# The order of all engines' calls in a four-block gated attention and mixture kernel

## The reference

```
x = x + tanh(g_xattn[0]) * cross_attention_0(layernorm(x), ctx)   # A: two softmax attentions, x to ctx and ctx-side, mixed by a sigmoid gate
x = x + tanh(g_ffn[0])   * moe_top1(layernorm(x))                 # B: softmax router over 8 experts, one 256x256 matrix of the best one
x = x + tanh(g_xattn[1]) * attention_1(layernorm(x), ctx)         # C: 16 heads of 16, rotary q and k, output projection
x = x + tanh(g_ffn[1])   * moe_top2(layernorm(x))                 # D: 8 experts of 256 to 128 to 256 with gelu, two best ones weighted
```

## Time and profile before

| | us |
|---|---|
| median of three runs | 514.29 (513.15 to 519.85) |
| the profiled execution | 510.58 |
| its span, first to last instruction | 509.3 |
| TensorE busy in it | 470.3 |
| VectorE, ScalarE, GpSimd busy | 356.2, 339.3, 272.5 |
| mean granted clock of TensorE | 0.97 |

### The profile page before, as it was taken

How to read it: one execution, slowest core, us unless ns; L and a number is a source line. 1 busy time by engine, 2 the same in 40 slices (tenths; PEclk the granted TensorE clock), 3 DMA queues, 4 the chain that set the end, 5 groups by cost and what they waited for, 6 DMA issues and landing times.

```text
span 509.3 us, 11112 instructions
## 1 busy us (share of the span) xinstructions
PE 470.3 (92%) x3918; PEld 409.2 (80%) x3918; DVE 356.2 (70%) x897; ACT 339.3 (67%) x691; POOL 272.5 (53%) x337
## 2 busy tenths in 40 slices
PE   3999999999999987589977699999999999999996
PEld 3899999989988877567745388698797978788896
DVE  6757876698636657957657878776774786975485
ACT  3587888748675633353264698888778768688843
POOL 2425563665624186764477767837666454432264
PEclk9999999979999995699999899999999999999999
DMA  7899200011456532779838160230500503000001
GB/s 206 287 352 363 105 23 2 23 62 63 126 156 194 188 107 86 221 204 310 246 119 266 43 217 17 100 93 1 170 23 3 190 22 127 26 2 24 1 23 41
DMA packets 41975, 61.51 MB, mean 121 GB/s; under 512 B 5198, under 2 KB 22976, under 8 KB 41920
## 3 DMA queue, kind: packets, MB, share of 16 engines
q1 hardware_dynamic: 36064, 52.67, 32.3%
q0 software_dynamic: 1536, 4.20, 2.7%
q10 hardware_dynamic: 4320, 3.93, 2.3%
HBM read 26.21 MB, written 17.43 MB: 86 GB/s over the span
## 4 chain that ended last, share of the span: by engine, by line
PE 71%; DVE 7%; POOL 6%; issue 5%; ACT 4%; DMA 4%; SPq 2%; POOLq 0%; ACTq 0%; DVEq 0%
PE psum L389 16%; PE psum L391 14%; PE psum L390 14%; PE psum L627 5%; PE psum L556 5%; PE psum L598 4%; PE psum L396 4%; PE psum L615 3%; ACT PT L1381 2%; DMA st<-parts 2%; POOL yg L2828 2%; PE psum L557 1%; SPq L3075 1%; PE psum L636 1%; DVE mpad L2261 1%
## 5 line engine op out<-in xcount | busy, mean ns | idle before, releaser
L2261 DVE TENSOR_REDUCE mpad<-psum 128x4 f32<-128x1024 f32 x64 | 76.7, 1219 | 22.0 <-PE psum L598 20.5
L1381 ACT ACTIVATE PT<-psum 128x1024 f32<-128x1024 f32 x64 | 64.2, 1024 | 20.6 <-PE psum L615 18.0
L2800 POOL TENSOR_TENSOR wA<-stage,wA 128x512 fp32r<-128x512 f32 x32 | 41.3, 1291 | 53.4 <-ACT wA L1428 50.9
L2330 DVE SCALAR_TENSOR_TENSOR xall<-psum,gat,xall 128x256 f32<-128x256 f32 x112 | 46.6, 476 | 7.1 <-PE psum L391 3.9
L389 PE MATMUL psum<-wB,wA 128*128 128x256 f32 x128 | 38.7, 302 | 0.1
L389 PE MATMUL psum<-x4h,wB 128*128 128x256 f32 x128 | 37.6, 294 | 0.0
L627 PE MATMUL psum<-PT,vv 128*32 128x256 f32 x512 | 35.1, 393 | 1.3 <-ACT PT L1381 1.3
L390 PE MATMUL psum<-wB,wA 128*128 128x256 f32 x128 | 35.9, 281 | 0.0
L391 PE MATMUL psum<-wB,wA 128*128 128x256 f32 x128 | 35.9, 280 | 0.0
L391 PE MATMUL psum<-x4h,wB 128*128 128x256 f32 x128 | 35.8, 279 | 0.0
L390 PE MATMUL psum<-x4l,wB 128*128 128x256 f32 x128 | 35.7, 279 | 0.0
(11 more groups left out here) (283 smaller groups left out, 1754.8 us busy)
## 6 DMA issues: line engine op xcount, KB each, us to landing
st<-parts SPq DMA_DIRECT2D x48, 256.0 KB, 3.0
wt<-exp_d SPq DMA_DIRECT2D x30, 256.0 KB, 2.8
slots_d<-ys SPq DMA_DIRECT2D x3, 2304.0 KB
stage<-mats_d SPq DMA_DIRECT2D x21, 256.0 KB, 3.9
cx<-ctx_d SPq DMA_DIRECT2D x16, 256.0 KB, 3.3
xs<-slots_d SPq DMA_DIRECT2D x30, 128.0 KB, 3.0
y_d<-ys ACTq DMA_DIRECT2D x30, 128.0 KB, 3.1
qr<-qp SPq DMA_DIRECT2D x28, 128.0 KB
```

The costliest lines, as they stand in the source:

```text
L1381: e.activation(PT[:, i:i + 2, :, :].rearrange("p a k n -> p (a k n)"), ps2("ST", b, j).rearrange("p a n -> p (a n)"), ACT.Exp, scale=0.25) ...
L2261: e.tensor_reduce(mpad[:, :, 0:16].rearrange("p t (o a) -> p t o a", a=8)[:, :, :, j], ps2("max", b, j).rearrange("p o (t n) -> p t o n", ...
L2330: e.scalar_tensor_tensor(out=xall[:, b, t, :], in0=ps("dn", b, x)[:, t * 256:(t + 1) * 256], scalar=gat[:, b % 2, t, x:x + 1], in1=xall[:, ...
L2800: e.tensor_tensor(hlo[:, i, :], stage[:, n % 4, :], hh[:, i, :].bitcast(F32), ALU.subtract).then_inc(h_lo, 1)
```

## The change

All five lists are written in another order. No helper changes, and each list holds the same calls as before. For TensorE a call may also write another PSUM bank than before (its last argument). Behind batch 4 of block C fewer calls move, and most lines of TensorE's diff there only change a bank. Where a call only changed its bank it does not count as moved. In batch 6 of block C, ACT adds the bias of the keys ahead of that of the queries, as in all other batches. The core of the diff, by engine:

```diff
@@ TensorE @@
 
             fold(0, 0)
-            ln_T("A", 0, 1)
-            fold_g(0, 2)
+            fold_g(0, 1)
+            ln_T("A", 0, 2)
             proj("t0", 0, 3)
             proj("vc", 0, 0)
             scores(0, 0, 1)
             fold(1, 2)
...
-            moe_T(14, 2)
+            ln_T("B", 5, 1)
+            moe_T(14, 3)
             moe_w(13)
             moe_w(14)
             rank(4, 0)
-            gate(7, 1)
+            route_B(5, 1)
+            gate(7, 2)
+            rank(5, 0)
+            mix(7, 1)
+            c_k(0, 2)
             ln_T("B", 6, 0)
-            c_k(0, 2)
-            route_B(6, 0)
-            mix(7, 1)
-            rank(5, 2)
-            rank(6, 3)
+            route_B(6, 1)
             ln_T("B", 7, 0)
             ln_T("C", 0, 1)
-            route_B(7, 2)
-            c_q(0, 0)
-            rank(7, 1)
-            c_v(0, 2)
-            ln_T("C", 1, 0)
+            route_B(7, 3)
+            rank(6, 0)
+            c_q(0, 2)
+            rank(7, 0)
+            c_v(0, 1)
+            ln_T("C", 1, 2)
+            c_q(1, 0)
             c_k(1, 1)
-            c_v(1, 0)
-            c_q(1, 1)
-            moe_T(15, 2)
+            c_v(1, 2)
+            moe_T(15, 1)
             moe_T(16, 3)
             moe_w(15)
...
+            c_exp(4, 0, 6)
             c_PV(1, 0)
-            c_exp(4, 0, 6)
             c_exp(5, 0, 4)
             c_exp(6, 0, 6)
             c_exp(7, 0, 4)
             c_PV(2, 0, 1)
             c_max(7, 1, 6)
             c_PV(3, 0)
-            c_maxT(1, 0)
-            c_out(0, 2, 1)
-            c_outT(0, 3)
-            c_v(3, 1)
+            c_v(3, 0)
+            c_out(0, 1, 2)
+            c_maxT(1, 3)
+            c_outT(0, 0)
             c_max(0, 2, 4)
@@ ScalarE @@
             store_tile(14)
             gate_t(7)
             x_hi("B", 6)
             top_exp(5)
-            k_bias(0)
             ln_apply("B", 7)
+            top_exp(6)
             ln_apply("C", 0)
             x_hi("B", 7)
+            k_bias(0)
             x_hi("C", 0)
-            top_exp(6)
             q_bias(0)
+            ln_apply("C", 1)
             ctx_hi("C", 1)
-            v_copy(0)
-            ln_apply("C", 1)
             x_hi("C", 1)
             part_hi(1, 0)
+            v_copy(0)
             part_hi(0, 0)
             k_bias(1)
+            xs_T(15)
             q_bias(1)
-            xs_T(15)
+            xs_T(16)
             ln_apply("C", 2)
...
+            store_tile(26)
             store_tile(25)
-            store_tile(26)
+            k_bias(3)
+            store_tile(27)
             xs_T(29)
-            store_tile(27)
             st_exp(0, 0)
+            st_exp(1, 0)
             store_tile(28)
-            st_exp(1, 0)
             store_tile(29)
             part_hi(0, 2)
             st_exp(2, 0)
             st_exp(3, 0)
-            k_bias(3)
             q_bias(3)
             st_exp(4, 0)
             st_exp(5, 0)
+            o_copy(0, 0)
             st_exp(6, 0)
             st_exp(7, 0)
-            o_copy(0, 0)
             o_copy(1, 0)
+            v_copy(3)
+            ctx_hi("C", 4)
             o_hi(0)
             ln_apply("C", 4)
-            ctx_hi("C", 4)
             st_exp(0, 1)
             part_hi(1, 3)
             st_exp(1, 1)
+            st_exp(2, 1)
             w_hi("f3")
-            w_hi("f0")
-            st_exp(2, 1)
             st_exp(3, 1)
             st_exp(4, 1)
             w_hi("f2")
             w_hi("f1")
+            w_hi("f0")
             st_exp(5, 1)
             x_hi("C", 4)
             st_exp(6, 1)
             ln_apply("D", 0)
             o_copy(0, 1)
...
             x_hi("C", 7)
+            k_bias(6)
             q_bias(6)
-            k_bias(6)
             ln_apply("D", 2)
@@ VectorE @@
             a_stats(7)
-            rcp(0, 4)
+            mixed(3)
             x_lo("A", 5)
-            mixed(3)
             rcp(1, 4)
+            slots(0)
             P_lo(0, 4)
-            slots(0)
+            proj_lo("t0", 5)
             proj_lo("vc", 4)
             P_lo(1, 4)
+            b_top(1)
+            proj_lo("t1", 5)
             gate_B(0)
-            b_top(1)
-            proj_lo("t0", 5)
-            proj_lo("t1", 5)
             slots(1)
             proj_lo("vs", 5)
+            gate_B(1)
             row_max(0, 5)
...
             slots(4)
+            w_lo("wv")
+            b_top(5)
             gated(7)
-            gate_B(5)
+            slots(5)
+            gate_B(4)
             mixed(7)
             add_moe(0)
             c_stats(0)
+            gate_B(5)
             b_top(6)
-            slots(5)
-            slots(6)
+            gate_B(6)
             add_moe(1)
             c_stats(1)
             x_lo("C", 0)
-            gate_B(6)
+            slots(6)
             b_top(7)
-            add_moe(2)
             slots(7)
             alloc(1)
+            add_moe(2)
             turned(1)
+            x_lo("C", 1)
+            c_stats(2)
             turned(0)
-            x_lo("C", 1)
             add_moe(3)
-            c_stats(2)
+            y_out(15)
             c_stats(3)
-            y_out(15)
@@ GpSimd @@
             ln_rstd("B", 3)
             scatter(0)
             ctx_lo("A", 6)
             out_lo(0, 4)
+            sum_diff(4)
             scatter(1)
-            sum_diff(4)
             out_lo(1, 4)
+            scatter(2)
             ln_rstd("A", 7)
             scatter(3)
-            scatter(2)
+            w_lo("r")
             out_lo(0, 5)
@@ SyncE @@
+            load("ks")
             load_ctx("A", 0)
-            load("ks")
             load("vs")
             load("vc")
             load_x(2)
             tables()
-            load_ctx("A", 1)
             load("kc")
             load("qs")
             load_x(1)
-            load_x(4)
             load("g1")
             load("g0")
+            load_ctx("A", 2)
             load_x(3)
+            load_x(4)
+            load_ctx("A", 1)
...
             load_tile(7)
+            load("f1")
             load_tile(8)
-            load_ctx("C", 1)
+            load("f3")
+            load("f0")
             load_tile(9)
             load_tile(10)
             load_tile(11)
+            load_ctx("C", 1)
             load_tile(12)
-            load_ctx("C", 2)
             load_tile(13)
             load_tile(14)
-            load("f3")
+            swap_half(1, 0)
+            load_ctx("C", 2)
             load("f2")
-            swap_half(1, 0)
             swap_half(0, 0)
+            load_tile(18)
             load_tile(16)
+            load_tile(15)
             load_tile(17)
-            load_tile(15)
-            load_tile(18)
             stack(0)
             swap_halves(1)
             load_tile(19)
             load_tile(20)
             load_tile(21)
+            load_ctx("C", 3)
             load_tile(22)
-            load_ctx("C", 3)
             load_tile(23)
             load_tile(24)
             load_tile(25)
             stack(1)
             load_tile(26)
+            swap_halves(2)
             load_tile(27)
-            swap_halves(2)
             load_tile(28)
             load_tile(29)
-            load("f0")
             max_rows(0)
             load_ctx("C", 4)
```

942 lines of the change are left out of this document (466 added, 476 removed).

## The result

The changed kernel took 511.88 us (median of 20 executions, 507.34 to 515.14) against 515.21 for the one before (20 executions beside it on the same chip): a ratio of 0.9939, 95% interval 0.9916 to 0.9963. That is 3.3 us less than the kernel before beside it (by the ratio 3.1 us of the 514.29 of the forecast), where 7.0 was forecast. The direction and the range held, the size did not.

What follows compares the result with a forecast made beforehand. The pool was taken as 24.6 us of TensorE idle time and 13.5 us of half clock, outside the full stage. Terms of -7.5 with 0.5 taken off gave -7.0: 514.29 to 507.3 us, range 500.0 to 515.5.

Steps and rivals of the forecast that it cites:

- 178 to 216 us: End of the first phase: earlier scatter(7) 1.0, C1's order and first tile's copy 1.0; -2.0 us, bounds -8.4 and +3.
- 216 to 296 us: Tiles and first attention: shorter ACT chain, earlier stack(2), one exponential put into a wait; -3.0 us, bounds -8 and +1.5.
- Start and the counts of batch 1: Earlier loads at the start, -0.3 us; at 101.8 to 116.0, TensorE's 0.7 us wait and a third of the clock, -2.2.
- the bound of this step: At 101.8 to 116.0, the upper bound of +1.2 us: another full GpSimd operation falling on another small one.
- that shorter longest gap may keep the clock up: At 178.2 to 216.0, c_k(0) behind mix(7) fills as much of the 5 us waiting there; no size of its own.
- third rival: Clock falls between gate(7) and mix(7), scatter(7) 3 us late if route_B(6) ends after 193.7; 517.3 us, chance 0.10.
- The seventh batch's keys: In the full stage, ACT's query bias waits 1.4 us for the keys' products, x_hi ahead of both; 0, bounds 0 and +0.8.
- the rest: The remainder of 296 to 509 us: 0, bounds -1.2 and +1.5 us.
- The base: Whole kernel: -7.0 us taken from the profiled execution of 510.58 us, carried over to the median of 514.29 us.
- the signs named: Right: one-hot waits within 1 us, half clock under 25, C1's ln_T 1 us sooner, stack(2) by 267.5. Wrong: new waits or half-clock stages.

Runs made afterwards that it cites:

- r13: The changed kernel a third time, in group 4, against the kernel before: ratio 0.9944, median 512.23 us.
- r9: The new order with c_k(0) moved between rank(5) and mix(7), in group 3, against the kernel before: ratio 0.9915, median 507.25 us.
- r14: The new order with c_k(0) between rank(5) and mix(7) once more, in group 4, against the kernel before: ratio 0.9894, median 509.08 us.
- r3: The changed kernel once more, for a second profile, against the kernel before: ratio 0.9933, median 513.30 us.
- r2: New order up to about 210 us (SP up to the eighth tile), old order behind it, against the kernel before: ratio 0.9981, median 514.88 us.
- r6: The new order with plain DMAs in place of all 16 indirect gathers, against the kernel before: ratio 0.9848, median 509.38 us.
- r4: The kernel before once more, unchanged, for a second profile: ratio 0.9999, median 516.83 us.
- r5: The old order with plain DMAs in place of all 16 indirect gathers, against the kernel before: ratio 0.9843, median 507.90 us.
- r11: The old order with plain DMAs in place of the gathers of batches 0 to 3, against the kernel before: ratio 0.9979, median 510.58 us.
- r17: The old order with plain DMAs in place of the gathers of batches 4 to 7, against the kernel before: ratio 0.9946, median 508.97 us.
- r12: The new order with plain DMAs in place of the gathers of batches 0 to 3, against the kernel before: ratio 0.9986, median 512.34 us.
- r18: The new order with plain DMAs in place of the gathers of batches 4 to 7, against the kernel before: ratio 0.9953, median 508.76 us.
- r7: The old order up to about 210 us, the new order behind it, against the kernel before: ratio 0.9984, median 515.77 us.
- r8: The kernel before with one edit, the bias of the seventh batch's keys ahead of its queries' on ACT: ratio 0.9999, median 515.73 us.

## Why the forecast was right or wrong, by its own steps

Two terms failed: 178 to 216 us (forecast -2.0, measured +0.3) and 216 to 296 us (forecast -3.0, measured -0.3). The same points in the profiles, in us (old: two; new: two; third, of r13, full clock 5 us late; c_k(0) moved: r9 and r14):

| | old | new | r13 | r9, r14 |
|---|---|---|---|---|
| moe_T(0) | 135.0, 135.0 | 133.2, 133.2 | 136.9 | 133.0, 133.2 |
| transposes of C1 | 209.2, 209.7 | 207.9, 208.0 | 213.2 | 206.1, 206.7 |
| st_exp(0, 0) | 258.8, 258.5 | 254.9, 257.5 | 261.9 | 254.0, 255.8 |
| st_exp(0, 2) | 311.2, 313.5 | 310.5, 310.5 | 315.9 | 305.9, 308.8 |
| end | 509.3, 511.5 | 508.5, 508.6 | 513.9 | 504.0, 507.3 |

- *Start and the counts of batch 1, -0.3 and -2.2.* -1.8 at moe_T(0), near the 2.5. The mechanism is as told, with the shares turned round: up to moe_T(0) half clock cost 3.4 us before and nothing in the first profile of the changed kernel, and TensorE's idle time rose from 10.0 to 10.8 us. The half clock went: none in r3 and r9 either, 3.4 us in r2, r6 and r13, against 6.8 in every profile of the old order. The wait did not: it moved to the counts of a later batch (1.86 at 114.83), and for the reason given as the bound of this step, another full GpSimd operation on another small one:

```profile
111.02 0.96 POOL L2817 DMA_INDIRECT slots_d<-xB,slot  x1 [0.30 <-issue]
112.01 1.28 POOL L2765 TENSOR_TENSOR cs1l<-cf,cs1h 128x512 fp32r<-128x512 f32 x1
...
111.58 1.75 DVE L2039 TENSOR_SCALAR sm<-sm 128x2 f32<-128x2 f32 x1
```

  The small operation ends at 113.33, when GpSimd's ends (113.29). By the Trainium skill, "SBUF — State Buffer", section "SBUF: two separate sides", the second comer is blocked for the whole instruction. The two ends agree with it; that VectorE's row begins 0.43 us ahead of GpSimd's, beside an indirect scatter, leaves open who came first.
- *178 to 216, -2.0: the first step that failed, by its mechanism.* The clause "that shorter longest gap may keep the clock up" is the wrong one: half clock began sooner and lasted longer. From moe_T(0) to C1's transposes, with TensorE's idle time and the price of half clock (half of the busy time that lies in it):

| | us | idle | price of half clock |
|---|---|---|---|
| old: before, r4 | 74.2, 74.7 | 8.7, 10.9 | 6.0, 4.1 |
| old, gathers replaced: r5, r11, r17 | 73.3, 73.3, 74.3 | 7.8, 7.8, 8.8 | 6.0, 6.0, 6.0 |
| new: first, r3, r13 | 74.6, 74.8, 76.3 | 7.9, 7.9, 7.9 | 7.1, 7.2, 8.9 |
| new, gathers replaced: r6, r12, r18 | 76.3, 74.8, 74.8 | 7.9, 7.9, 7.9 | 8.9, 7.2, 7.2 |
| c_k(0) moved: r9, r14 | 73.0, 73.5 | 9.0, 9.3 | 3.9, 4.1 |

  Less both, 59.5 to 60.1 us are left in each of the thirteen profiles, so these two account for the lengths. The new order took idle time off (0.8 us against the first profile, 3.0 against r4, whose idle time holds the late increments) and paid for it with half clock, 23.9, 27.3 and 30.7 us of it against 20.5 and 17.0 (stretches that begin in the stage). What brings it is in the forecast's third rival (with nothing between gate(7) and mix(7) the clock falls before c_k(0) and route_B(6)); I had priced that as all or nothing, deciding at 193.7. route_B(6) ended at 191.0, well before that, so the rival's 3 us did not come, but its half clock did. With the wait filled the price falls by 3.1 to 3.2 us for 1.1 to 1.4 us more of idle time: r9 and r14 are 1.4 us faster here than the first two profiles of the new order, and 1.2 faster than the old, not the full 2.0 of the forecast. The Trainium skill, "TensorE: Matmul & The Clock Gate", section "Part 1: The HAM clock gate", has idle time take the clock down; the trace agrees in part. Here a wait of 1.79 us in a thinly filled stretch was followed by half clock within 1 us of its end in the first profile, r3, r12 and r18. It is not the whole cause: in r13 and r6 a first half-clock stretch of 3.4 us began 6.6 us before the end of that wait, and in r2, with the same wait, half clock came only at 191.9, 5.4 us behind it:

```profile
186.48 0.66 PE L512 MATMUL psum<-ident,uu 128*128 128x128 f32 x4 [1.79 <-DVE uu L2056]
```

- *216 to 296, -3.0: the second step that failed; what took it is open.* One part came as forecast. From the first exponential to the issue of stack(2) it was 10.21 us and is 8.76 (263.69): 1.45 sooner, forecast 1.5, and 5.3 in all with what came before. But from C1's transposes to st_exp(0, 2) the old profiles take 102.0 and 103.8, the new ones 102.6, 102.6 and 102.7, so -0.3 in the mean is what is left of -3.0. In the changed kernel there are the 3.61 us of wait, beside the gathers, and 6.8 us of half clock from 267.9, for which the forecast has no term. They are not shown to be what took the gain: where no profile of either order has a late increment, the same piece takes 98.2 us old and 98.7 new (r5, r6), 103.0 and 102.7 (r11, r12), 99.2 and 99.0 (r17, r18), so there the gain is no larger. r7, the new order from 216 on alone, gave nothing either. In the first profiles stack(2) is issued 5.3 us sooner and st_exp(0, 2) starts only 0.7 sooner.
- *The seventh batch's keys, 0*, and *the rest, 0*: right (r8; 198.0 to 198.1 us from st_exp(0, 2) to the end in the two old and three new profiles).
- *The base.* "510.58 - 7.0 = 503.6 ... 514.29 - 7.0 = 507.3 by the same difference" took the profiled execution for a typical one. It had 30.7 us at half clock and no late increment; its kernel's mean was 41 to 43 on three chips and 32 to 33 on a fourth. So the profiles of old and new differ by 0.8 and 2.9 us (1.9 between the means of the first two each), and the medians by 3.3: some of the measured gain lies in what my one profile could not show, and for that part the forecast's sign was luck. The late mix(7) and rank(5), which three profiles of the old order (r4, r7, r8) have at 188 to 196, are a part of it that I can name, but did not isolate; in the three profiles of the changed kernel the reader of mix(7) starts at once (185.96 in the first, behind 185.92).

Of the signs named: the start of the C1 transposes, stack(2) and the full stage came as for a right forecast; a wait for the counts over 1 us, 39.2 us at half clock in the profile instead of under 25, and half clock in 178 to 192 and 262 to 277 came as for a wrong one.

The terms sum to -7.5; the first two profiles of each order show -1.8 + 0.3 - 0.3 = -1.8. Over the whole span TensorE's idle time was 39.0 and 39.7 us in them, and is 36.7 and 37.8 (37.0 in r13): 2.1 us off, 2.2 with r13, less than a third of the forecast. Half clock cost 13.5 and 15.6 us, and costs 15.4 and 14.0 (18.9 in r13), where the forecast counted on less.

The version with c_k(0) in the wait is 4.1 us (r9) and 5.9 us (r14) faster than the kernel before, by the medians, and 3.2 us faster than the changed kernel on the one chip that timed both.

Open: what in an indirect DMA holds TensorE's increments back, and why on some chips; what took the 3.0 us of 216 to 296; the changed kernel on the chip that shows no late increments (the three pairs of orders with gathers replaced say 0.2 us faster to 1.8 us slower than the old one by the medians, but none is the kernel itself); and what the pause at 265 costs, since r17 and r18 met a chip without it.

## What to carry to other kernels

Split every execution into time at half clock and the rest before and after a reordering. An order that packs the idle time of a thin stretch can make TensorE's clock fall earlier, and each us of half clock in which TensorE is busy gives back half a us (27.0 of 30.7 us before and 30.8 of 39.2 after, in the profiles); ask first which short wait now stands bare, and put a call that is ready there, even if it waited nowhere before. And take a second profile of the kernel before: its first was 4.6 us faster than its median, and a forecast built on it had too little half clock in it.

## What the runs showed of the hardware

TensorE's increments came 0.4 to 3.6 us late only while GpSimd issued indirect DMAs back to back (scatters at 122 to 125 and 200 to 203, gathers at 186 to 196 and 261 to 276 us), never in the full stage, and in none of the six profiles of one chip. The longest ended 1.1 to 1.3 us behind the last DMA of the series that was being issued (266.31 and 267.43 in the changed kernel; 190.76 and 192.04 in r4). The same kernel was 511.3 us on that chip and 515.0 to 515.9 on three others, with some 10 us less at half clock. And the moment at which full clock first comes, 11 or 16 to 17 us, moves a whole execution by up to 2 us.
